# Two swaps in VectorE's instruction order in an attention and expert kernel: the turned probabilities' low part ahead of the sums, the row maximum ahead of queries' and keys' low part

## The reference

```python
x = x + xattn(layernorm(x), ctx)
#   q = xn @ Wq;  k, v = split(ctx @ Wkv);  p = softmax(q k^T / 8)   (128 x 128 per head and sequence)
#   xattn = (p v) @ Wproj + bproj
x = x + ffn(layernorm(x))
#   top2 of softmax(xn @ gate^T);  e_out = silu(xn @ expert_w[e]^T + expert_b[e])
#   ffn = (sum over the two chosen e of weight * e_out) @ combine_w^T
```

## Time and profile before

| what | value |
|---|---|
| median of 3 runs | 1564.38 us (1560.76 to 1565.78) |
| profiled execution: its own time | 1562.21 us |
| its span | 1560.20 us |
| PE busy | 1504.2 us, 96% |
| DVE busy | 1283.8 us, 82% |
| ACT busy | 1071.8 us, 69% |
| POOL busy | 939.8 us, 60% |
| mean granted clock of TensorE, share of full speed | 0.991 |

### The profile page before, as it was taken

One profiled execution on the slowest core, in us unless ns is written; L12 is line 12 of the kernel. 1 busy time (PEld: TensorE's weight loads), 2 busy tenths in 40 slices (PEclk: granted clock), 3 DMA queues, 4 the chain that ended last, 5 costly groups with the idle time before them and its releaser, 6 DMA issues.

```text
span 1560.2 us, 38495 instructions
## 1 busy us (share of the span) xinstructions
PE 1504.2 (96%) x11680; PEld 1440.2 (92%) x11680; DVE 1283.8 (82%) x3129; ACT 1071.8 (69%) x2929; POOL 939.8 (60%) x1237
## 2 busy tenths in 40 slices
PE   6999999999999999999999999999999999999878
PEld 5889999999899999999899999989999999999767
DVE  7888888888888888878888888898888888877556
ACT  5766677777667766777677676767776767767545
POOL 4666666666555655587666455576676556655624
PEclk9999999999999999999999999999999999999989
DMA  6643433333577777455688777658788777877813
GB/s 189 196 150 95 120 96 96 96 95 102 167 225 229 220 219 217 118 129 149 176 242 239 208 225 223 180 154 241 233 245 237 238 218 238 264 225 222 299 52 115
DMA packets 181595, 287.78 MB, mean 184 GB/s; under 512 B 23696, under 2 KB 116880, under 8 KB 181136
## 3 DMA queue, kind: packets, MB, share of 16 engines
q1 hardware_dynamic: 170640, 255.94, 57.0%
q0 software_dynamic: 10752, 29.37, 5.9%
HBM read 156.51 MB, written 61.60 MB: 140 GB/s over the span
## 4 chain that ended last, share of the span: by engine, by line
PE 73%; DVE 12%; issue 6%; ACT 3%; SPq 2%; POOL 2%; DMA 1%; DVEq 0%; ACTq 0%; POOLq 0%
PE gen_ps L592 20%; PE qk_ps L592 16%; PE o_ps L592 10%; PE proj_ps L592 9%; PE s_ps L592 9%; PE pT_ps L633 6%; PE gen_ps L711 2%; DVE sums L1070 2%; PE gen_ps L678 1%; DVE neg_max L1063 1%; DVE pT_s_lo L1005 1%; PE gen_ps L686 1%; DMA k_s<-qk_s 1%; POOL stage L1438 1%; DVE xn L1050 1%
## 5 line engine op out<-in xcount | busy, mean ns | idle before, releaser
L1402 POOL CAST o_s_hi<-stage 128x256 fp32r<-128x256 f32 x256 | 102.5, 401 | 413.9 <-ACT stage L822 413.1
L848 ACT ACTIVATE stage<-s_ps,neg_max 128x128 f32<-128x128 f32 x1024 | 293.1, 373 | 74.7 <-DVE neg_max L1063 73.3
L1393 POOL TENSOR_TENSOR stage<-stage,inv_sums 128x512 f32<-128x512 f32 x256 | 266.7, 1042 | 11.7 <-DVE inv_sums L1072 11.7
L822 ACT CAST pT_s_hi<-pT_ps 128x512 fp32r<-128x512 f32 x256 | 150.8, 589 | 130.2 <-PE pT_ps L633 129.3
L592 PE MATMUL s_ps<-k_s,qk_s 128*128 128x256 f32 x1536 | 226.0, 283 | 3.6 <-DMA k_s<-qk_s 2.3
L1070 DVE TENSOR_REDUCE sums<-stage 128x4 f32<-128x512 f32 x256 | 172.8, 675 | 44.5 <-ACT stage L848 43.0
L592 PEld LDWEIGHTS s_ps<-k_s,qk_s 128*128 128x128 f32 x1536 | 201.1, 189 | 4.5 <-DMA k_s<-qk_s 2.8
L1005 DVE TENSOR_TENSOR qk_s<-qk_ps,qk_s 128x512 fp32r<-128x512 f32 x256 | 176.2, 688 | 31.0 <-ACT qk_s L822 26.1
L1404 POOL TENSOR_TENSOR o_s_lo<-stage,o_s_hi 128x256 fp32r<-128x256 f32 x256 | 188.8, 738 | 20.8
L1005 DVE TENSOR_TENSOR pT_s_lo<-pT_ps,pT_s_hi 128x512 fp32r<-128x512 f32 x256 | 171.8, 671 | 30.8 <-ACT pT_s_hi L822 28.7
L822 ACT CAST v_s_hi<-gen_ps 128x512 fp32r<-128x512 f32 x129 | 75.8, 587 | 176.5 <-PE gen_ps L592 176.5
(11 more groups left out here) (367 smaller groups left out, 4696.5 us busy)
## 6 DMA issues: line engine op xcount, KB each, us to landing
w_block<-expert_table SPq DMA_DIRECT2D x147, 512.0 KB
k_s<-qk_s SPq DMA_DIRECT2D x512, 128.0 KB
stage<-sorted_x SPq DMA_DIRECT2D x147, 128.0 KB, 2.5
sorted_y<-stage SPq DMA_DIRECT2D x147, 128.0 KB
x_raw<-in_x SPq DMA_DIRECT2D x32, 256.0 KB
c_raw<-in_ctxT SPq DMA_DIRECT2D x32, 256.0 KB, 3.3
stage<-in_x SPq DMA_DIRECT2D x32, 256.0 KB, 3.6
x_kept<-x SPq DMA_DIRECT2D x32, 256.0 KB, 3.8
```

Of the source, the lines that this page charges most:

```text
L822: last = act.copy(to, of)
L848: last = act.activation(probs[p % 2][:, k, :], s_ps[:, k * P:(k + 1) * P], ACT.Exp, bias=neg_max[p % 2][:, k:k + 1])
L1393: pool.tensor_tensor(probs[b][:, :, :], probs[b][:, :, :], inv_sums[b][:, :].unsqueeze(2).broadcast_to([P, 4, P]), ALU.mult).then_inc(prob ...
L1402: pool.tensor_copy(hi[:, :, :], o_full).then_inc(o_hi, 1)
```

## The change

In VectorE's loop over the slots, `inverse` of this slot's head pair and `pT` of the one before change places, so that `pT` comes first; further down, `row_max` and `qk` change places, so that `row_max` comes first. Nothing else is touched: no instruction is added or taken away, and the lists of the other engines are the same as before.

```diff
                 now, before, nxt = exists(i), exists(i - 1), exists(i + 1)
-                if now:
-                    inverse(i, u)
                 if u == 0 and before:
                     pT(i - 1, 7)
                 if u > 0 and now:
                     pT(i, u - 1)
+                if now:
+                    inverse(i, u)
                 if u == 2 and before:
                     add_residual(i - 1)
...
                 if s - 3 in plan.mix:
                     combined(plan.mix[s - 3])
+                if u < 7 and now:
+                    row_max(i, u + 1)
+                if u == 7 and nxt:
+                    row_max(i + 1, 0)
                 if u < 5 and now:
                     qk(i, u + AHEAD)
                 if u >= 5 and nxt:
                     qk(i + 1, u - 5)
-                if u < 7 and now:
-                    row_max(i, u + 1)
-                if u == 7 and nxt:
-                    row_max(i + 1, 0)
                 general(s, "early")
```

## The result

The changed kernel takes 1575.56 us (median of 5 runs, 1574.23 to 1578.35), beside 1564.38 for the kernel before (5 runs, 1560.50 to 1565.78): a ratio of 1.0082, 95% interval 1.0068 to 1.0095. It is slower by 11.2 us where 3.8 were forecast, just beyond the range.

The account below looks back on a forecast made before the run. TensorE, busy 96% of the span, was taken as the bound. Costs of 13.8 us less gains of 10.0 gave +3.8 us, 1568.2 us on the median 1564.4; the 8-in-10 range was 1561 to 1575 us.

Parts of the forecast that it names:

- Net 13 x 0.33 = 4.3 us: End of slot 6, 13 places mostly in pairs without expert blocks: earlier `pT` ends TensorE's wait, 4.3 us gained.
- at nothing outside the places above: All slots: the later inverse costs nothing beyond the named places, as GpSimd splits the attended values first.
- The term of slot 2: Slot 2, 9 pairs with blocks and combinations: sums behind `pT` delay `expert_out` by 0.81 us each, 7.3 us cost.
- Slot 4 (0.35 each): Slot 4 of the same 9 pairs: `expert_out` comes 0.36 us later and TensorE waits, 3.2 us cost.
- the pairs with blocks and no combination: 8 pairs: `rest_lo`, due at slot 5, comes later; 0.15 us each reaches TensorE, 1.2 us cost.
- the gain at 1222 and 1319 us: Two waits behind `count_blocks`: TensorE gains the full 0.81 us at each; with 744 us, 2.4 us.
- the gain at 392 and 1027 us: Two waits behind `count_blocks` where GpSimd waits for the later inverse: about 0.35 us gained each, 0.7 us together.
- 744 us: Wait behind `count_blocks`: gap falls from 2.05 to 1.24 us, gaining 0.81, plus 1.6 us of clock (bounds 0 and 1.6).
- the cost of the start: Program start: low part of queries and keys, and key copy, come later; 1.4 us cost (bounds 0.6 and 3).
- the second swap counted as nothing or a cost: `row_max` ahead of `qk`: no gain counted; costs 1.4 us at the start and part of 0.7 at the end.
- Rival A: Slower outright: costs spread, as each late `expert_out`, inverse or key copy can open a TensorE gap; 1572 us, chance 0.25.
- Rival B: Faster: earlier exponentials pull the high part, so `expert_out`'s 18 waits don't grow; -6.7 us, 1557.7 us, chance 0.10.

Follow-up runs that it names:

- the three kernels that have its code up to 59 us at least: Against the kernel before: first swap in slots 2 and 4 beside expert blocks (1573.98 us); both swaps in slots 7 and 6 (1561.61); that plus `count_blocks` (1557.88).
- the first four kernels: Against the kernel before: first swap alone (1580.93 us); second alone (1563.97); both, second not before the first pair (1578.08); both, sums first beside expert blocks (1565.97).
- the last two: Against the kernel before: both swaps in slot 7 alone (1559.99 us); the same, first swap also behind `count_blocks` of pairs 17, 27, 29 (1556.83 us).

## Why the prediction was wrong

Two steps failed. The gain of slot 7 was booked net of nearly nothing ("Net 13 x 0.33 = 4.3 us"), and the later inverse and what follows it were costed "at nothing outside the places above". In their place the runs showed 3.7 us of loss behind slots 3 and 5, and 2.3 us less gain than forecast at four of the `count_blocks` places (392, 1027, 1222 and 1319 us).

**Right: the mechanism and place of the cost.** Slots 2 and 4 beside combinations hold most of the loss, at the nine places named, by the sums that come between `pT` and `expert_out`. Shown from both sides: that swap alone costs 9.7 us, and without the swaps beside blocks the change costs 1.1 us (ratio 1.0007). The term of slot 2 was a tenth too small, 0.89 and not 0.81 a place: `expert_out` now starts 2.10 and not 1.20 + 0.81 us behind `pT`. Slot 4 (0.35 each) and the pairs with blocks and no combination (0.15 estimated, 0.18 measured, but nine of them and not eight) came out nearly as sized.

**Wrong: "Net 13 x 0.33 = 4.3 us".** The gain at slot 7 is real, 0.25 to 0.34 in 12 places and 0.15 in a thirteenth, but the step that the other slots of these pairs give nearly nothing back failed. I had named the place (slots 3 to 5, "some 0.10 us of new idle time") and then left it out of the sum. Pairs 2 to 8 lose 0.09 each behind slot 3, where the inverse is late for GpSimd (the waits of `pT_ps` for it rose from 17 to 41), and 0.13 behind slot 5 at queries and keys: 1.5 us together. Swapping in slot 7 alone brings the 0.27 and no such loss: shown.

**Wrong: nothing "outside the places above".** Pairs 16 and 17, with combinations and no blocks, lose 0.3 behind slot 3 and 0.66 behind slot 5, 1.9 us together, and had no term at all. The first swap alone loses about as much there by the end of slot 4 (0.9 each), the second alone nothing. The loss at slot 5 is the step of slot 4 once more: in pair 16 `rest_lo` started 3.21 us behind `pT` and now starts 3.91 behind it, as the sums stand between. TensorE's load, before and after:

```profile
718.19 0.19 PEld L592 LDWEIGHTS qk_ps<-xT_hi,wq_s_hi 128*128 128x128 f32 x1 [0.49 <-issue]
```
```profile
722.22 0.19 PEld L592 LDWEIGHTS qk_ps<-xT_hi,wq_s_hi 128*128 128x128 f32 x1 [1.20 <-issue]
```

With 0.3 in pairs 9 and 15 this makes the 3.7 us. What the loss behind slot 3 of pairs 16 and 17 hangs on was only read from the trace.

**Wrong: the gain at 1222 and 1319 us.** `o_ps` waits 0.79 less there, as predicted (1.55 to 0.76). But the combination's weights (`wcomb`) then wait 0.46 us for `xbT_lo`, which stands behind the moved sums on VectorE: the net is 0.23. TensorE's load in the changed kernel:

```profile
1230.72 0.19 PEld L592 LDWEIGHTS o_ps<-pT_s_hi,v_s_hi 128*128 128x128 f32 x1 [0.76 <-DVE pT_s_lo L1005]
...
1233.38 0.19 PEld L592 LDWEIGHTS gen_ps<-wcomb_s_hi,mT_s_hi 128*128 128x128 f32 x1 [0.46 <-DVE xbT_lo L1005]
```

**Wrong: the gain at 392 and 1027 us.** The step was right for its own slot (0.33 won, 0.35 forecast) and blind to the next two, which give back 0.60. GpSimd's late multiplication is followed by a late inverse of the next slot; this chain is read from the trace and was not tested by a run of its own.

**Right, in part by luck: 744 us.** 0.8 of the gap and 1.6 of clock: 2.35 measured. The gap by the PE rows is 1.21 us now, beside 2.05. But of the five kernels that keep the long gap at this place (1.70 to 2.05 us) the clock fell in three and stayed in two: that the profiled execution of before had the fall is partly luck, and so is the full 1.6 us.

```profile
747.53 0.39 PE L592 MATMUL o_ps<-pT_s_hi,v_s_hi 128*128 128x256 f32 x1 [1.21 <-DVE pT_s_lo L1005]
```

**Not borne out: the cost of the start.** The booked 1.4 us didn't show, as told above, and no run isolates them to that size. I added to the median what I had worked out against the profiled execution. The profiled times differ by 13.4 us and the medians by 11.2, because the profiled execution of before was 2.2 below its median; its first two pairs were 2.1 to 2.8 us faster than those of the three kernels that have its code up to 59 us at least.

**Wrong: the second swap counted as nothing or a cost.** Alone it is nothing (0.9997). With the first it is what passes slot 7's gain on: 0.03 without it in that slot, 0.27 with it. Rival A had the sign and named the spreading, and its mark, over 4 us of new waits of TensorE for the inverse through GpSimd, came just so (4.2 for `pT_ps`); its time of 1572 was too low as well. Rival B's condition, an earlier high part beside the blocks, did not come: the idle time before `pT_s_lo` there is 2.67 us.

## What to carry to other kernels

Work that is ready early and stands ahead of an instruction with a late input is a filler. Before moving it behind, list which late inputs it covers, and which later instruction of the stage is due next. If two late inputs follow each other, ready work can cover only the one that it stands ahead of. Make such a swap only in the stages where the engine arrives late and the input is already there, and move with it whatever the next engine in the loop waits for. A gain at one wait must be followed at least two stages on.

## What the runs showed of the hardware

**The clock after a gap is not decided by the gap's length alone.** At the three waits behind `count_blocks` (392, 744 and 1027 us), gaps of 1.7 us or more on the PE rows stand in 19 places of the twelve traces; behind 5 of them the granted clock fell from 2.4 to 1.2 GHz for a while (0.83 on average over 10 us), at a cost of 1.1 to 1.6 us. Behind the other 17 gaps, of under 1.4 us, it never did. The same gap of 2.00 us, first in the kernel with the swap only beside experts, with its stretch:

```profile
747.13 0.39 PE L592 MATMUL o_ps<-pT_s_hi,v_s_hi 128*128 128x256 f32 x1 [2.00 <-DVE pT_s_lo L1005]
```
```profile
743.00:753.00 10.00, 8.00 (x51) 0.83 0.36 108
```

and in the one with the swaps in slots 7 and 6:

```profile
746.55 0.38 PE L592 MATMUL o_ps<-pT_s_hi,v_s_hi 128*128 128x256 f32 x1 [2.00 <-DVE pT_s_lo L1005]
```
```profile
743.00:753.00 10.00, 8.00 (x59) 1.00 0.30 90
```

Equal gaps and equal busy time in the window, one with the fall and one without. The Trainium skill (page "TensorE: Matmul & The Clock Gate", section "What's actually happening") has the activity judged by a window that runs on its own, not from the gap's start. In that these traces agree: a gap's length doesn't settle it. A trace with one fall is therefore an example and not a fixed cost: of the 1.6 us at 744 only a share is won on average.

**ScalarE paused for no recorded reason.** In six of the ten experiments it stands still for some 0.5 to 1.5 us before one instruction at the same few places (mostly in pairs 15 to 17, 23 and 30), although its input was long there; in the other four, and in the profiles of before and after, never. With the second swap left out at the start, TensorE's last matmul into `qk_ps` ends at 688.94 us, and ScalarE, idle since then too, takes it out 1.5 us later:

```profile
688.66 0.28 PE L592 MATMUL qk_ps<-cT_hi,wkvr_s_lo 128*128 128x256 f32 x1
```
```profile
690.44 0.59 ACT L822 CAST qk_s<-qk_ps 128x512 fp32r<-128x512 f32 x1 [1.49 <-PE qk_ps L592]
```

and the same instruction, with the same code on ScalarE, in the changed kernel:

```profile
690.27 0.59 ACT L822 CAST qk_s<-qk_ps 128x512 fp32r<-128x512 f32 x1
```

The kernel with the second swap left out at the start differs from the changed one only in the slots before the first pair, and falls 5.3 us behind it between pairs 15 and 31, where these pauses are. Those with pauses ran in two groups, each on a chip of its own (the first four kernels, and the last two), those without on a third. ScalarE's code isn't the reason; whether the chip is, or something else, stays open. The medians of the kernel before are alike in all groups (1563.8 to 1564.6). So spans of profiles from different groups are compared here only place by place, and never where a pause stands; part of the 5.4 us by which the median of the first swap alone is above that of both may be pauses.
